# Linear attention over eight groups of tokens: two places per buffer, an own order of steps on each engine, and the softmax sums applied behind the key products

## The reference, cut to what matters

```python
Q  = ln(x @ Wq + bq, gq, betaq)      # K and V alike; ln = layer norm over the 128 features
K  = concat([zeros, Kc]); V = concat([zeros, Vc])          # one leading row of zeros
phi_Q = tanh(Q @ Wfq + bfq) + 1;  phi_K = tanh(K @ Wfk + bfk) + 1
q_probe = mean(Qh, tokens) / sqrt(8)
score = softmax(einsum('bhd,bhkd->bhk', q_probe, Kh))      # one weight per key and head
pKw  = pK * score[..., None]
KV   = einsum('bhkd,bhke->bhde', pKw, Vh);  Ksum = sum(pKw, keys)
out  = einsum('bhqd,bhde->bhqe', pQ, KV) / (einsum('bhqd,bhd->bhq', pQ, Ksum) + 1e-6)
a    = ln(out, ga, ba)
h    = a + (gelu(a @ W1 + b1) @ W2 + b2);  return h + x
```

## Time and profile before

| what | value |
|---|---|
| time, 3 runs | 4153.27 us median (4149.71 to 4153.57) |
| the profiled execution's own time | 4150.1 us |
| its span | 4148.3 us |
| mean granted TensorE clock | 0.956 |
| busy, share of the span | PE 91%, DVE 77%, ACT 69%, POOL 52% |
| linear attention | from 55.83 us (first project) to 293.09 us (end of the last addition into `yT`) |

### The profile page before, as it was taken

One profiled execution on the slowest core, in us unless ns is written; L12 is line 12 of the kernel. 1 busy time (PEld: TensorE's weight loads), 2 busy tenths in 40 slices (PEclk: granted clock), 3 DMA queues, 4 the chain that ended last, 5 costly groups with the idle time before them and its releaser, 6 DMA issues. The chain is left out here.

```text
span 4148.3 us, 185380 instructions
## 1 busy us (share of the span) xinstructions
PE 3768.5 (91%) x68782; PEld 2970.3 (72%) x68782; DVE 3198.1 (77%) x9882; ACT 2868.2 (69%) x8525; POOL 2169.6 (52%) x2238
## 2 busy tenths in 40 slices
PE   4556999998999989999899998999989999599997
PEld 3333788867888678886788866888678886377773
DVE  4644788877888778887788877888778887588883
ACT  2223788856888568885688856888568885388883
POOL 2211677746777467774677746777467772300000
PEclk7767999999999999999999999999999999799998
DMA  1000333323333233332333322333223331100000
GB/s 38 1 5 27 79 79 79 81 61 76 79 79 80 62 77 78 80 80 63 75 80 80 79 66 74 80 80 79 66 73 80 80 80 43 34 0 0 0 0 26
DMA packets 305306, 246.34 MB, mean 59 GB/s; under 512 B 74485, under 2 KB 299860, under 8 KB 304340
## 3 DMA queue, kind: packets, MB, share of 16 engines
q1 hardware_dynamic: 305108, 243.72, 23.3%
HBM read 24.54 MB, written 2.12 MB: 6 GB/s over the span
## 5 line engine op out<-in xcount | busy, mean ns | idle before, releaser
L810 ACT ACTIVATE wa_pb<-wa_sc,wa_nm 128x64 f32<-128x64 f32 x3072 | 670.3, 329 | 405.9 <-DVE wa_nm L1006 405.9
L1156 POOL TENSOR_TENSOR wa_t<-wa_t,wa_rn 128x512 f32<-128x512 f32 x768 | 785.1, 1043 | 278.5 <-DVE wa_rn L984 277.8
L1162 POOL TENSOR_TENSOR wa_t<-wa_t 128x512 f32<-128x512 f32 x384 | 495.3, 1290 | 500.6 <-DVE wa_t L960 500.5
L958 DVE TENSOR_TENSOR wa_t<-wa_pj,wa_ctab 128x512 f32<-128x512 f32 x768 | 526.9, 686 | 260.5 <-PE wa_ta L572 215.5
L44 PE MATMUL wa_pj<-lw_wqkv_high,wa_xhigh 128*128 128x512 f32 x1152 | 540.4, 469 | 76.2 <-issue 41.2
L793 ACT ACTIVATE wa_sq<-wa_pj 128x512 f32<-128x512 f32 x768 | 489.6, 639 | 131.6 <-PE wa_pj L46 129.9
L1171 POOL TENSOR_TENSOR wa_t<-wa_t 128x512 f32<-128x512 f32 x384 | 490.6, 1278 | 0.0
L46 PE MATMUL wa_pj<-lw_wqkv_high,wa_xlow 128*128 128x512 f32 x1152 | 465.8, 404 | 0.0
L45 PE MATMUL wa_pj<-lw_wqkv_low,wa_xhigh 128*128 128x512 f32 x1152 | 463.6, 402 | 0.0
L966 DVE TENSOR_REDUCE wa_raw<-wa_sq 128x16 f32<-128x1024 f32 x384 | 449.2, 1170 | 0.0
L640 PE MATMUL wa_ob<-wa_oT,wa_wo 128*128 128x128 f32 x3072 | 406.8, 276 | 1.0 <-DVE wa_on L1018 0.8
(11 more groups left out here) (262 smaller groups left out, 8664.7 us busy)
## 6 DMA issues: line engine op xcount, KB each, us to landing
wa_vv<-wa_vt SPq DMA_DIRECT2D x2304, 65.0 KB
wa_vv<-wa_vt SPq DMA_DIRECT2D x1152, 32.5 KB
lw_wqkv<-L_ffn_Wqkv SPq DMA_DIRECT2D x6, 1536.0 KB
lw_xs<-yT SPq DMA_DIRECT2D x96, 64.0 KB, 1.9
lw_fs<-yT SPq DMA_DIRECT2D x48, 128.0 KB
lw_xs<-yT SPq DMA_DIRECT2D x96, 63.8 KB, 2.0
lw_fs<-yT SPq DMA_DIRECT2D x96, 63.8 KB
wa_wo<-L_ffn_Wo SPq DMA_DIRECT2D x6, 512.0 KB, 4.0
```

The costliest lines, as they stand in the source:

```text
L810: last = nc.scalar.activation(pb[:, u.par(2), p, e, :], SC[:, e, p * KEYS:(p + 1) * KEYS], ACT.Exp, bias=nm[:, u.par(2), e, p:p + 1])
L958: nc.vector.tensor_tensor(t1[:, b, j], x, table(ctab, slice(0, HD)), ALU.mult)
L1156: nc.gpsimd.tensor_tensor(here, here, rn[:, u.par(1), j * HG:(j + 1) * HG].unsqueeze(2).broadcast_to((128, HG, HD)), ALU.mult).then_inc(s. ...
L1162: nc.gpsimd.tensor_tensor(t1[:, b, 0], t1[:, b, 0], t2[:, b, 0], ALU.add).then_inc(s.qadd_done, 1)
```

## The change

Only `linear_attention` is changed, and two helpers are new. What it does:

- All steps are written out (`spelled`, as the layer norms have it), with no loop. Each engine has its own list: `LA_PE`, `LA_ACT`, `LA_DVE`, `LA_POOL`, cut into finer steps, with lags of 0 to 6, so that up to seven groups are under way.
- Nearly every SBUF buffer gets two places (`u.par`), and the waits for a free place look two groups back (`standing(..., u, 2)`).
- The PSUM banks are shared between steps; `vacated` waits for the reader that used the bank last.
- Normalising V (4 of the 12 tiles) and normalising `ao` go from DVE (subtract, multiply) to ACT (scale and bias). For it DVE makes minus mean times deviation once per group (`neg`, `neg2`).
- The exponentials and the zero row's weight are no longer multiplied by the reciprocal of their sum. PE spreads the reciprocals with the same small matmul (4 columns in place of 2), and DVE multiplies by them where it masks `KV` (two instructions of 128x128 in place of one of 128x256) and where it makes the denominators' columns.
- POOL makes the deviations of Q and K apart from those of V, and takes over the addition into `yT`.

```diff
+LA_PE = [("R2", 1), ("K", 3), ("F1", 2), ("F0", 2), ("P0", 0), ("P1", 0), ("C0", 1), ("R0", 0), ("S", 2), ("C1", 1),
+    ("R1", 0), ("T", 2), ("D0", 3), ("D1", 3), ("P2", 0), ("L", 1), ("Z", 5)]
+LA_ACT = [("a", 6), ("e", 2), ("t1", 2), ("t0", 2), ("c0", 0), ("an", 5), ("c1", 0), ("q0", 1), ("q1", 1), ("vn", 1),
+    ("c2", 0)]
+LA_DVE = [("s0", 0), ("sc", 2), ("pr", 1), ("s1", 0), ("pk", 2), ("g01", 0), ("d", 3), ("mx", 1), ("pl", 2), ("nm",
+    1), ("s2", 0), ("ao", 3), ("kx", 2), ("g2", 0), ("nb2", 4), ("n0", 0), ("w", 1), ("n1", 0), ("nb", 0), ("st2", 3)]
+LA_POOL = [("rA", 0), ("rV", 0), ("y", 5), ("vt", 1), ("r2", 3)]
+def vacated(eng, u, *readers):
+    for sem, lag, *per in readers:
+        if 0 <= u.at - lag < NGRP:
+            standing(eng, sem, u, lag, *per)
+            return
...
+        bank = [ps(f"b{i}") for i in range(8)]
+        PJ, RW, CL = [bank[2], bank[4], bank[1]], [bank[7], bank[3], bank[5]], [bank[1], bank[0]]
+        FT, ND = [bank[0], bank[1]], [bank[2], bank[0]]
+        LG, TK, TS, KV, AN = bank[6], bank[4], bank[6], bank[4], bank[1]
...
+                def feature(n):   # PE, F0 and F1
+                        standing(pe, qk_out[n], u, 0, SPG if n == 0 else 1)
+                        vacated(pe, u, *(
+                                       ((s.ao_done, 2), (qk_out[1], 0), (tanh_done[0], 1)),
+                                       ((s.a_out, 4), (col_out[2], -1), (qk_out[0], 0, 2), (tanh_done[1], 1)))[n])
...
+                def turn_scores(u):   # PE, S
+                    standing(pe, s.rc_done, u)
+                    nc.tensor.matmul(TS[:, TPG * HEADS:TPG * HEADS + 2 * SPG], hselT[:, :],
+                                     zr[:, u.par].rearrange("h a q -> h (a q)"), start=True, stop=True)
...
+                def value_rows(u):   # ACT, vn; an is the same with ao, neg2 and rstd2
+                    standing(act, s.neg_v, u)
+                    standing(act, s.vt_scaled, u, 2)
+                    for t in range(TPG):
+                        last = nc.scalar.activation(row[:, u.par, 2, t, :], tiles(RW[2])[:, t, :], ACT.Identity,
+                                                    bias=neg[:, u.par, t:t + 1],
+                                                    scale=rstd[:, u.par, 2 * TPG + t:2 * TPG + t + 1])
...
+                def shift_v(u):   # DVE, nb; nb2 is the same with mv2 and rstd2
+                    nc.vector.scalar_tensor_tensor(out=neg[:, u.par, :], in0=mv[:, u.par, 2 * TPG:3 * TPG, 0], scalar=-1.0,
+                                                   in1=rstd[:, u.par, 2 * TPG:3 * TPG], op0=ALU.mult, op1=ALU.mult)
+                def totals(u):   # DVE, w
+                    nc.vector.tensor_tensor(tot[:, u.par, :], tot[:, u.par, :], zr[:, u.par, 0, :], ALU.add)
+                    nc.vector.reciprocal(zr[:, u.par, 1, :], tot[:, u.par, :]).then_inc(s.rc_done, 1)
-                    nc.vector.tensor_tensor(s0[:, :], z0[:, :], rc[:, :], ALU.mult).then_inc(s.s0_done, 1)
-                    nc.vector.tensor_tensor(ex[:, :, :], ex[:, :, :], rc[:, :].unsqueeze(2).broadcast_to(
-                        (HEADS, SPG, SEQ)), ALU.mult).then_inc(s.ex_done, 1)
...
+                    for q in range(SPG):   # DVE, kx
+                        nc.vector.scalar_tensor_tensor(out=kvx[:, u.par, q, 0:D], in0=kv[:, q, 0:D],
+                                                       scalar=sct[:, u.par, inverse + q:inverse + q + 1], in1=hmask[:, :],
+                                                       op0=ALU.mult, op1=ALU.mult)
+                    for q in range(SPG):
+                        last = nc.vector.tensor_scalar(kvx[:, u.par, q, D:D + HEADS], hsel[:, :], ks[:, q:q + 1],
+                                                       sct[:, u.par, inverse + q:inverse + q + 1], ALU.mult, ALU.mult)
...
+                def residual(u):   # POOL, y
+                    standing(pool, s.a_out, u)
+                    nc.gpsimd.tensor_tensor(yT[:, u.cols()], yT[:, u.cols()], aT[:, u.cols()], ALU.add).then_inc(s.y_out, 1)
```

More of the change, by code:

```diff
@@ L1309, in _ @@
                 pe.wait_ge(s.loaded, ALL_LOADED)
[L1311 to L1347, removed]
+                def transposes(out, src, done):
+                    for t in range(TPG):
+                        last = nc.tensor.transpose(out[:, t * D:(t + 1) * D], src(t), ident[:, :])
+                    last.then_inc(done, 1)
@@ L1351, in feature, with turn_keys @@
                     last.then_inc(s.logits_done, 1)
-                def weigh(u):
-                    pe.wait_ge(s.tanh_done, u.count(2, 2))
-                    for t in range(TPG):
[L1357 to L1364, removed]
+                def turn_keys(u):
+                    standing(pe, tanh_done[1], u)
+                    vacated(pe, u, (col_out[1], -2), (s.kvx_done, 1), (s.pkw_done, 1))
+                    transposes(TK, lambda t: phi[:, u.par, 1, t * D:(t + 1) * D], s.pk_turned)
@@ L1368, in sum_ @@
                 def sum_(u):
-                    pe.wait_ge(s.pkw_done, u.count(1, 1))
-                    pe.wait_ge(s.vt_ready, u.count(1, 1))
+                    standing(pe, s.pkw_done, u)
+                    standing(pe, s.vt_ready, u)
+                    vacated(pe, u, (s.pkw_done, 0), (col_out[1], -2), (s.kvx_done, 1))
                     for q in range(SPG):
[L1373 to L1376, removed]
+                        for tt in range(half):
+                            t = q * half + tt
+                            last = nc.tensor.matmul(KV[:, q * (D + 1):(q + 1) * (D + 1)], pkw[:, u.par, t, :],
+                                                    vt[:, u.par, t, :], start=(tt == 0), stop=(tt == half - 1))
@@ L1390, in finish, with divide, step @@
[L1390 to L1397 removed]
+                def divide(q):
+                    def step(u):
+                        standing(pe, s.kvx_done, u)
+                        standing(pe, s.plus1, u)
+                        vacated(pe, u, *(
+                                       ((col_out[0], -3), (s.ao_done, 1)),
+                                       ((qk_out[1], -2), (tanh_done[0], -1), (s.ao_done, 1)))[q])
+                        for tt in range(half):
+                            t = q * half + tt
+                            last = nc.tensor.matmul(ND[q][:, tt * (D + HEADS):(tt + 1) * (D + HEADS)],
+                                                    phi[:, u.par, 0, t * D:(t + 1) * D], kvx[:, u.par, q, :], start=True, stop=True)
+                        last.then_inc((s.num0_done, s.num1_done)[q], 1)
+                    return step
@@ L1436, in finish, with normalise @@
+                def normalise(u):
+                    standing(act, s.neg2_done, u)
+                    standing(act, s.an_turned, u, 2)
+                    for t in range(TPG):
+                        last = nc.scalar.activation(an[:, u.par, t, :], ao[:, u.par, t, :], ACT.Identity,
+                                                    bias=neg2[:, u.par, t:t + 1], scale=rstd2[:, u.par, t:t + 1])
+                    last.then_inc(s.an_done, 1)
                 def finish(u):
-                    act.wait_ge(s.an_turned, u.count(1, 1))
```

406 lines of the change are left out of this document (241 added, 165 removed).

## The result

The changed kernel takes **4025.3 us**, the median of four executions (4021.39 to 4037.71), against 4153.4 for the kernel before on the same chip (four, 4149.71 to 4156.46). The ratio is 0.9697, interval 0.9674 to 0.972.

A forecast was written before the change was run, and what follows sets the result against it. The stage was taken as bound by its chain's latency, DVE next: 4.4 + 26.1 + 70.0 + 22.8 = 123.3 us, plus 3 for the clock, 126 in place of 237.3; 4153.3 - 111 = 4042 us, range 4030 to 4063.

The forecast's parts named there:

- the rival with PE at 0.50: Clock stays low in the stage and PE bounds it: in part 4058 us, 15%; at 0.50 throughout 4094 us, 2%.
- a broken tie: Rival: waits between the engines' lists exceed their 0.5 us slack, each turn loses 2 to 4 us: 4057 us, 14%.
- The full turn, forecast 14.0: Steady part of the stage: DVE's 13.4 us plus 0.6 for holds, in place of 27.3; five such turns, 70.0 us.
- Some fifteen hand-overs: Inside DVE's turn: 0.03 to 0.05 us left between two instructions brings 13.0 us to some 13.4.
- from below: Low end of DVE's turn, 12.3 us: independent small instructions start before the one ahead has ended.
- Holds, forecast 0.6 per turn: DVE instructions waiting beside POOL's large ones: two of some 0.3 us per turn, ends 0 and 2.5.
- the prediction's other figure: Holds by the skill's exclusive-lock rule, each to the end of POOL's instruction: 1.3 us per turn, sum 3.5 us longer.
- Fill and drain: Stage time outside the five full turns: 56.3 us, with 3 (between 0 and 6) for PE's low clock.
- The rest is the same: Everything outside the linear-attention stage unchanged, so the stage's gain of 111 us is taken from the median 4153.3.
- the lower end, 4030: Range's fast end: DVE's turn at 12.3 us, no holds, no clock loss; stage 115, total 4031, taken to 4030.
- ACT, POOL, PE: Work per steady turn: ACT 10.1 us, POOL 8.0, PE 11.2 at full clock; ACT's 128x128 instructions 448 ns each.
- the turn from which the change loses: Slower-than-before rival, 1%: the change loses from about 27.4 us per turn; example total 4166 us.

The follow-up runs named there:

- two edits in the old order: Kernel before, with the addition into `yT` on POOL and the reciprocals applied where `KV` is masked: 4133.9 us, ratio 0.9957, stage 218.5 us.
- norms_on_dve: Changed kernel with the normalisings of V and `ao` back on DVE, out of ACT's list: 4048.6 us, ratio 0.9746, turn 15.0, stage 135.7 us.
- nb_late: Changed kernel with nb (minus mean times deviation) moved behind the second statistics in DVE's list: 4023.2 us, ratio 0.9699, stage 115.1 us.
- nb_clear: Changed kernel with POOL's two large `vt` instructions moved behind the second deviations, last in its list: 4028.1 us, ratio 0.9702, stage 118.5 us.
- nb_one_input: Changed kernel with nb as four one-column `tensor_scalar` instructions in place of one with two SBUF inputs: 4033.2 us, ratio 0.9702, turn 12.37 us.
- the second profile: Changed kernel run again unchanged, in a second series: 4035.5 us, ratio 0.9712, stage 121.0 us.
- sums_before: Changed kernel with the reciprocals multiplied in before the key products again and masking as one instruction: 4034.1 us, ratio 0.9713, stage 125.7 us.
- old_order_y_pool: Kernel before, with only the addition into `yT` moved to POOL: 4143.2 us, ratio 0.9976, stage 227.9 us.
- the runs with P0 twice: First projection matmul issued twice per group, in the changed kernel and in nb_late: 4049.05 and 4049.6 us, one execution each.
- nb_late_p0_twice: nb_late with the first projection matmul issued twice per group: 4049.6 us, one execution.

## Why the prediction was right in kind and wrong in size

- **What bounds it, and what takes its place**: right. The chain was the bound (two edits in the old order bring a stage of 218 us, the new order brings 136 without the normalisings on ACT and 120 with them), DVE took its place (`norms_on_dve`), the clock went to 1.00 by itself, the rival with PE at 0.50 did not occur, nor did a broken tie.
- **The full turn, forecast 14.0: wrong, 12.87.** This is the step that failed inside the stage: "DVE's turn is then ... 13.0 us. Some fifteen hand-overs ... bring it to some 13.4". Without its hold the turn is 11.9 to 12.0 (`nb_late`). The prices of the edits held in sum. Adding up DVE's groups of instructions in one turn gives 17.2 us before (116.55 to 143.85) and 13.7 to 13.9 in `nb_late`: 3.4 less, where 16.55 - 13.0 = 3.55 was forecast. What failed is the overlap. Before, the union of DVE's work in that turn (16.6) is 0.6 below the sum of its groups; in `nb_late` it is 11.9, so 1.8 to 1.9 below. The starts and ends of neighbours of different groups say the same: they overlap by 0.8 us per turn before and by 2.0 to 2.1 in the changed kernel and in `nb_late`. As I read it, in the old chain many neighbours waited for each other or for another engine, while in the new lists more of them are independent: the next one starts up to 0.1 us before the one ahead has ended (n1 ends at 111.19 and nb starts at 111.10). The prediction named this, gave 12.3 as the end "from below", and charged hand-overs in place of it. The sign was wrong: DVE sits idle for 0.1 us per turn (12.87 - 12.77), and the overlap gives back more than that.
- **Holds, forecast 0.6 per turn:** 0.95, all by one instruction. The term was too small, and the prediction's other figure, with both held to the end of POOL's instruction (1.3), too large, because w fell beside no large POOL instruction: its sum starts 0.08 us before `yT`'s addition or `vt` and takes 0.14, a matter of luck in the layout (in `norms_on_dve` it meets the addition and is held for 1.0). The Trainium skill (SBUF — State Buffer, Who interferes with whom) says that a DVE instruction with two SBUF inputs contends with a GpSimd instruction that reads SBUF. The runs agree for nb where it is held (1.06 to 1.16 us) and for w and the product on 16x2; they don't for w beside POOL's power (0.14), and nb runs beside `vt` in `nb_late` without a hold (0.13). The same section of the Trainium skill names `tensor_scalar` as well among the operations that can contend; nm in `nb_clear` is one and was held for 1.13 us, as the pair of the earlier trace rows was before, while the four of one column in `nb_one_input` were not (0.56 together).
- **Together:** the first four full turns have 12.87, the fifth, behind which no s0 comes, 11.3: 62.8 us against 70. Fill and drain 56.8 against 56.3 with the 3 for the clock. Stage 119.5, in the second profile 121.0, against 126: 5 to 6.5 of the 17 us. That fill and drain agree is partly luck: a hold of nb lies in the fill (86.43) and one of the denominators' columns, of 1.3 us, in the drain (157.20), which the prediction didn't charge.
- **The other 10 us, the larger part of the miss: "The rest is the same" was wrong as a figure.** The code behind the stage is the same, but takes a different time in each execution. The local-attention layers, in four profiles, in order the kernel before, after, `sums_before` and `old_order_y_pool` (columns as in the earlier trace rows):

```profile
386.10:3604.20 3218.10, 3024.73 (x64220) 2470.94 (x64220) 2609.79 (x6823) 2340.22 (x6801) 2090.57 (x2138) 0.98 0.30 74
```

```profile
270.00:3490.20 3220.20, 3025.14 (x64222) 2474.37 (x64222) 2609.25 (x6823) 2341.38 (x6801) 2091.47 (x2138) 0.98 0.29 74
```

```profile
275.10:3484.80 3209.70, 3014.36 (x64220) 2463.16 (x64220) 2612.36 (x6823) 2341.41 (x6801) 2091.51 (x2138) 0.98 0.30 74
```

```profile
377.00:3601.60 3224.60, 3031.32 (x64220) 2476.78 (x64220) 2612.00 (x6823) 2343.69 (x6801) 2091.09 (x2138) 0.97 0.29 74
```

  The same instructions take 3209.7 to 3224.6 us; PE's busy time moves by the same amount and in the same direction (3014 to 3031), while DVE, ACT and POOL differ by 3.5 us at most. What changes is how long PE stands at its low clock. By the clock's records it stands at 0.50 for 153.5, 158.4, 125.1 and 169.7 us of these four stretches; in the second series of the changed kernel the mean granted clock was 0.971 in the fastest execution (4028.75 us) and 0.966 in the slowest (4043.27).

  Everything outside the stage took 3903.4 to 3927.6 us over all profiles; the two longest are the runs with P0 twice, and the clock doesn't explain those (at 0.50 for 225 and 222 us behind the stage, in the profile of after for 232). In the profile of after it was 5 us longer than in that of before (3916.3 against 3911.0), in three experiments 3 to 8 us shorter. So the gain between the two profiled executions, 112.4, meets the forecast of 111 by luck: 118 from the stage, less 5 outside it.

  The nine executions of the changed kernel lie between 4021.4 and 4043.3, with a median of 4030.2; the three fastest of the nine are among the first four. Corrected for the stage alone the forecast would have been 4036; the lower end, 4030, was worked out from the stage and left nothing for this spread, which is the reason why the median fell below it. That the nine together lie 0.2 us inside is luck as well. The stage of before, too, was taken from one profile (237.3; the second has 231.2). Whether the rest is also a little shorter as a rule behind the new stage stays open.
- **ACT, POOL, PE:** right. vn 462 and an 481 ns (forecast 448), spaced 0.38 and 0.41 us (0.35); ACT 9.8 per turn (10.1), POOL 7.9 (8.0), PE 10.9 to 12.3 (11.2).
- **Two slips in the sums**, which moved nothing that matters: the turn from which the change loses is, by the prediction's own 26 us for fill and drain, (237.3 - 26) / 8 = 26.4 and not 27.4 us; and turn 2 of the fill is 8.5 + 2.4 = 10.9 with the terms given, not 10.3.

The version with the shortest stage is `nb_late`, one entry of one list moved: 115.1 us against 119.5 and 121.0; the totals don't tell it apart. In its turns of 12.0 us DVE is busy for 11.9 and PE for up to 11.8, so I'd expect less work on one of them alone to bring little; this wasn't tried.

## What to carry to other kernels

When a stage is bound by a chain over engines, lay the steps of several groups side by side with one list per engine, and expect the turn of the fullest engine; take its work as the union, not the sum, since independent neighbours overlap: without the hold the turn came out 1.4 us under the sum that charged hand-overs. With lists, the place of one tiny instruction is a free choice worth 7% of a turn: keep DVE instructions with two SBUF inputs, and `tensor_scalar` ones that read and write SBUF, out from beside POOL's large ones, and with some distance, since in `nb_late` with P0 twice nb started 0.02 to 0.03 us later behind POOL's instruction and the hold was back. And a forecast of a total needs the spread of the code that isn't changed in its range, here some 15 to 20 us between the fastest and slowest execution of a kernel.

## What the runs showed of the hardware

- A DVE instruction of 4 columns with two SBUF inputs that starts during POOL's 128x512 mostly lasts to the end of POOL's: 1.09 us in place of 0.14. On 16 partitions and 2 columns the same (1.01; w in `norms_on_dve` 0.98). In four instructions of one column with the second factor as a scalar operand nothing is held (205 ns each), while nm, 16x2 from SBUF to SBUF with one input, was held (1.13), and so was a 128x16 of the denominators' columns in the drain (1.3 in place of 0.28).
- It goes the other way too: POOL's 128x512 took 1.79 in place of 1.27 beside DVE's 16x512 product (0.67) in `sums_before`, and 1.46 in place of 1.18 beside `phi` plus one (0.41) in `nb_clear`. Of two that start within 0.1 us of each other the recorded starts don't tell which one is held: nb started 0.03 us (`after`) and 0.08 us (`nb_late_p0_twice`) behind POOL and was held, 0.05 us behind in `nb_late` and was not.
- POOL's power (1.01 us on 128x4) held nothing: w's sum, with two SBUF inputs, starts and ends within it and takes 0.14. In the changed kernel:

```profile
84.07 1.01 POOL L1691 TENSOR_TENSOR la_rstd<-la_rstd,mhalf 128x4 f32<-128x4 f32 x1
84.89 0.14 DVE L1589 TENSOR_TENSOR la_tot<-la_tot,la_zr 16x2 f32<-16x2 f32 x1
```

- 0.86 us of additional matmul work per turn of 12.87 was free behind the first full turn, at a clock of 1.00.
- The same 64220 matmuls take 3014 to 3031 us of PE's busy time in four profiles, with a mean granted clock of 0.97 to 0.98 and 125 to 170 us at 0.50.
